# Causal attention on one core: VectorE's work placed behind TensorE's, a second part buffer, merged narrow steps, and products for the maxima issued twice

## The reference, cut to what matters

```python
B, L, D, H = (32, 64, 512, 32)     # x itself is (2, 1024, 512)
HD = D // H
q = (x @ Wq.T + bq).reshape(b, l, h, hd).transpose(0, 2, 1, 3)
k = (x @ Wk.T + bk).reshape(b, l, h, hd).transpose(0, 2, 1, 3)
v = (x @ Wv.T + bv).reshape(b, l, h, hd).transpose(0, 2, 1, 3)
scores = jnp.einsum('bhqd,bhkd->bhqk', q, k) / math.sqrt(hd)
scores = jnp.where(causal, scores, -jnp.inf)
att = jax.nn.softmax(scores, axis=-1)
out = jnp.einsum('bhqk,bhkd->bhqd', att, v)
out = out.transpose(0, 2, 1, 3).reshape(b, l, d) @ Wo.T + bo
```

## Time and profile before

| | us |
|---|---|
| median of three runs | 4300.12 (4286.41 to 4308.26) |
| the profiled execution, in all | 4294.83 |
| its span | 4293.1 |
| TensorE busy | 3861.4 (90%) |
| VectorE busy | 2711.2 (63%) |
| GpSimd busy | 1880.8 (44%) |
| ScalarE busy | 1695.2 (39%) |
| mean granted TensorE clock | 0.907 of full |
| attention, first batch (first projection to last turn) | 29.2 to 477.2 |
| attention, second batch | 2173.7 to 2617.4 |

### The profile page before, as it was taken

One profiled execution on the slowest core, in us unless ns is written; L12 is line 12 of the kernel. 1 busy time (PEld: TensorE's weight loads), 2 busy tenths in 40 slices (PEclk: granted clock), 3 DMA queues, 4 the chain that ended last, 5 costly groups with the idle time before them and its releaser, 6 DMA issues.

```text
span 4293.1 us, 61464 instructions
## 1 busy us (share of the span) xinstructions
PE 3861.4 (90%) x18056; PEld 2813.5 (66%) x18056; DVE 2711.2 (63%) x5034; ACT 1695.2 (39%) x3538; POOL 1880.8 (44%) x2017
## 2 busy tenths in 40 slices
PE   7899799689999999979878896996899999999797
PEld 4444478567777777757654444885677777777576
DVE  3567445577777777764435673555777777777644
ACT  1344411355545555541113444113555555555411
POOL 1111344355555655654311113443555556655542
PEclk8677899899999999989977767998999999999899
DMA  3221011011100111001032210110101001110010
GB/s 73 36 36 31 24 51 45 22 33 30 32 20 25 34 32 29 22 15 45 35 81 36 36 32 29 46 45 22 35 28 32 20 25 34 32 29 22 15 52 35
DMA packets 81456, 145.59 MB, mean 34 GB/s; under 512 B 16392, under 2 KB 18520, under 8 KB 81264
## 3 DMA queue, kind: packets, MB, share of 16 engines
q1 hardware_dynamic: 81264, 143.28, 12.9%
HBM read 113.08 MB, written 4.19 MB: 27 GB/s over the span
## 4 chain that ended last, share of the span: by engine, by line
PE 69%; issue 11%; DVE 7%; ACT 4%; POOL 3%; DVEq 2%; POOLq 2%; DMA 1%; SPq 1%; ACTq 0%
PE banks L492 15%; PE banks L493 14%; PE banks L494 14%; PE banks L832 4%; PE banks L671 4%; PE banks L652 3%; PE banks L628 3%; PE banks L825 2%; PE banks L845 2%; DVE conv L1344 2%; DVEq L1347 1%; PE banks L767 1%; PE banks L768 1%; POOL X L1509 1%; ACT conv L1005 1%
## 5 line engine op out<-in xcount | busy, mean ns | idle before, releaser
L1344 DVE SCALAR_TENSOR_TENSOR conv<-banks,cpar,conv 128x509 f32<-128x509 f32 (+2 forms) x576 | 428.2, 744 | 115.3 <-ACT conv L1005 100.9
L948 ACT ACTIVATE probs<-banks 128x1024 f32<-128x1024 f32 (+3 forms) x384 | 297.7, 810 | 309.4 <-PE banks L652 308.9
L1172 DVE TENSOR_TENSOR Y<-banks,Y 128x512 f32<-128x512 f32 x400 | 276.1, 691 | 188.1 <-PE banks L494 187.9
L1608 POOL TENSOR_SCALAR_AFFINE_SELECT probs<-probs 128x256 f32<-128x256 f32 x256 | 104.2, 408 | 645.8 <-ACT probs L948 645.5
L628 PE MATMUL banks<-stack_k,stack_q 48*128 48x512 f32 (+3 forms) x768 | 331.7, 502 | 59.3 <-DVEq L1218 19.8
L1672 POOL TENSOR_TENSOR state<-state,gt 128x512 f32<-128x512 f32 x112 | 133.5, 1192 | 500.4 <-PE banks L825 500.4
L492 PE MATMUL banks<-xhi,f_hi 128*128 128x512 f32 x800 | 322.6, 403 | 3.5 <-DVE xlo L1143 3.5
L492 PE MATMUL banks<-xhi,wx_hi 128*128 128x512 f32 x768 | 312.0, 406 | 14.4 <-DVE conv L1344 14.4
L493 PE MATMUL banks<-xhi,f_lo 128*128 128x512 f32 x800 | 319.9, 400 | 0.0
L494 PE MATMUL banks<-xlo,f_hi 128*128 128x512 f32 x800 | 319.4, 399 | 0.0
L494 PE MATMUL banks<-xlo,wx_hi 128*128 128x512 f32 x768 | 306.0, 398 | 0.0
(11 more groups left out here) (209 smaller groups left out, 10185.0 us busy)
## 6 DMA issues: line engine op xcount, KB each, us to landing
m_raw<-in_w_mamba SPq DMA_DIRECT2D x224, 256.0 KB, 2.6
f_raw<-in_w_ffn SPq DMA_DIRECT2D x50, 768.0 KB, 4.5
stack_q<-part_hi SPq DMA_DIRECT2D x128, 64.0 KB, 2.4
stack_k<-part_hi SPq DMA_DIRECT2D x128, 64.0 KB, 2.5
X<-in_x SPq DMA_DIRECT2D x4, 1024.0 KB, 6.5
wqk_raw<-in_w_attn SPq DMA_DIRECT2D x8, 512.0 KB, 3.5
stack_q<-part_lo SPq DMA_DIRECT2D x64, 64.0 KB, 2.4
stack_k<-part_lo SPq DMA_DIRECT2D x64, 64.0 KB, 2.5
```

Of the source, the lines that this page charges most:

```text
L948: act.activation(probs[n % 2][:, 2 * p:2 * p + 2, 0:w], banks[:, 2 * p:2 * p + 2, 0:w], ACT.Exp, scale=1.0 / HD ** 0.5).then_inc(exp_done[ ...
L1172: dve.tensor_tensor(Y[:, i, :], bank[6 + i % 2], Y[:, i, :], ALU.add).then_inc(f["dn_used"], 1)
L1344: r = dve.scalar_tensor_tensor(out=rest, in0=src[:, 0:HALF - lag], scalar=cpar[:, o:o + 1], in1=rest, op0=ALU.mult, op1=ALU.add)
```

## The change

Seven edits in attention, made together.

1. STEPS: the last two key tiles of each half become one step, with both tiles' scores side by side in one bank (`blocks`), one exponential and two masks: ten steps a quad instead of twelve.
2. VectorE's and ScalarE's parts get entries of their own (`proj_hi`, `proj_lo`, `values_out`, `maxima_out`, `turn_out`) that stand later in the order than TensorE's; a projection is issued in two halves of six matmuls in two consecutive steps. Banks are assigned ahead (`ring_banks`), and each use waits for the release of what that bank held last; before the first scores seven banks take part instead of three.
3. The parts get a second buffer, in the memory of X; x is loaded again at the end of attention, and POOL waits for that before it adds.
4. Projections move: the two of k of f = 1 from before the first scores into quad 0, those of f = 2 into quads 0 and 1, those of f = 3 into quads 2 and 3 (`PROJ_STEPS`).
5. Each head's stack DMAs have a semaphore of their own, and TensorE waits per head. SP's list is reordered: `stack(t + 1)` before `put_maxima(t)`.
6. From quad 1 on every piece is issued twice in a row, with the same operands into the same bank; in quad 7, which has no pieces to go with, every score is.
7. `maxima t + 1` still comes in the last step but one, pieces are dealt out over ten steps.

The diff, cut to its core:

```diff
-                part_hi = sb("part_hi", [P, 2, L], F32R, stack=s2)
-                part_lo = sb("part_lo", [P, 2, L], F32R, stack=s2)
+                part_hi = [sb("part_hi", [P, 2, L], F32R, stack=s2)[:]]
+                part_lo = [sb("part_lo", [P, 2, L], F32R, stack=s2)[:]]
+                for part, h in ((part_hi, 0), (part_lo, 1)):
+                    own = X[:, h * CPH:(h + 1) * CPH, :].rearrange("p (w u) d -> p w (u d)", w=2)
+                    part.append(own.bitcast(F32R))
...
-        STEPS = [(s, j) for s in range(2) for j in range(CPH * (s + 1))]
+        STEPS = [(s, (j,) if j < CPH * (s + 1) - 2 else (j, j + 1)) for s in range(2) for j in range(CPH * (s + 1) - 1)]
...
+        MAIN_BANKS, FIRST_BANKS = (4, 5, 7), (4, 5, 7, 0, 1, 2, 3)
+        for f, use, t, n in ((1, 2, 0, 0), (1, 3, 0, 2), (2, 0, 0, 6), (2, 1, 1, 0), (2, 2, 1, 3), (2, 3, 1, 6),
+                             (3, 0, 2, 2), (3, 1, 2, 6), (3, 2, 3, 0), (3, 3, 3, 4)):
+            PROJ_STEPS[t, n], PROJ_STEPS[t, n + 1] = (f, use, 0), (f, use, 1)
...
             for use in range(4):
-                yield "proj", 0, use
-            for i in range(5):
+                yield from project(0, use)
+            for i in range(2):
                 yield "values_in", i
+                yield "values_out", i
             for n in range(NP):
-                if n in (3, 9, 15):
-                    yield "values_in", 5 + (n - 3) // 6
-                if n in (21, 27, 33, 39):
-                    yield "proj", 1, (n - 21) // 6
-                yield "piece", 0, n
+                if n % 6 == 3 and n < 36:
+                    yield "values_in", 2 + n // 6
+                if n % 6 == 2 and 2 < n < 42:
+                    yield "values_out", 1 + n // 6
+                if n in (36, 40, 43, 46):
+                    yield "proj", 1, int(n > 40), int(n in (40, 46))
...
                     for q in range(QUAD):
                         yield "score", t, n, q
                         if n == NS - 2 and q == 1 and t + 1 < NQ:
                             yield "maxima", t + 1
+                        turning = n == NS - 2 and q < 2 and t + 1 < NQ
+                        more = n < NS - 2 and q == 0 or n in (0, 4) and q == 2
+                        yield from some(0 if turning else 2 if more else 1)
+                        if n == NS - 2 and q == 2 and t + 1 < NQ:
+                            yield "maxima_out", t + 1
+                        if q == 1 and n == 3 and t > 0:
+                            yield "turn_out", t - 1, 1
+                        if q == 1 and n == 7:
+                            yield "turn_out", t, 0
+                        if q == 2 and (t, n - 2) in PROJ_STEPS and PROJ_STEPS[t, n - 2][2]:
+                            yield "proj_lo", *PROJ_STEPS[t, n - 2][:2]
                     if n > 0:
                         yield "values", t, n - 1
-                    if n == 1 and t > 0:
+                    if n == 2 and t > 0:
                         yield "turn", t - 1, 1
-                    if n == 7:
+                    if n == 6:
                         yield "turn", t, 0
...
 # TensorE
-                        pe.wait_ge(ring_free, b * RING + ring - 2)
-                        r = pe.matmul(dst[:, 0:cols], stack_q[buf][base:base + ROWS, h, i * P:(i + 1) * P],
-                                      stack_k[buf][base:base + ROWS, h, s * HALF:s * HALF + cols],
-                                      start=True, stop=True)
+                        if i == 0:
+                            pe.wait_ge(stacked[t % 2][h], (b * (NQ // 2) + t // 2 + 1) * STACKED)
+                        bank_free(BEFORE[use])
+                        for _ in range(1 if t == 0 else 2):
+                            r = pe.matmul(bank[RING_BANK[use]][:, 0:cols],
+                                          stack_q[buf][base:base + ROWS, h, i * P:(i + 1) * P],
+                                          stack_k[buf][base:base + ROWS, h, s * HALF:s * HALF + cols],
+                                          start=True, stop=True)
...
+                        for j, lo, at, w in blocks(n) * (2 if t == NQ - 1 else 1):
+                            r = pe.matmul(bank[h][:, at:at + w],
...
 # SP
-                stack(0)
-                stack(1)
-                load_qk(1)
-                held(sp, v_used, b + 1)
-                ones_in(1)
-                put_maxima(0)
-                load_qk(2)
+                load_qk(1)
+                stack(0)
+                stack(1)
+                put_maxima(0)
+                load_qk(2)
+                held(sp, v_used, b + 1)
+                ones_in(1)
                 stack(2)
...
+                for t in range(2, NQ):
+                    if t + 1 < NQ:
+                        stack(t + 1)
                     put_maxima(t)
...
+                for par in range(2):
+                    for h in range(QUAD):
+                        held(sp, stacked[par][h], (b + 1) * (NQ // 2 * STACKED))
+                load_x(b)
                 leave(sp, b, ATT)
...
 # POOL
-            def add_normed(e, e_next):
+            def add_normed(e, e_next, b=None):
                 for i in range(TT):
+                    if b is not None and i % CPH == 0:
+                        held(pool, x_in[i // CPH], b * 32 + 32)
```

More of the change, by code:

```diff
@@ L299, in attention_order @@
+                if n == 45:
+                    yield "proj_lo", 1, 0
+                yield from some(1)
+            yield "maxima", 0
+            yield from some(2)
+            yield "maxima_out", 0
+            yield from some(2)
+            yield "proj_lo", 1, 1
+            yield from some(AHEAD - 4)
             for t in range(NQ):
@@ new lines, in build, with release @@
+        FREES = [o for o in ORDER if o[0] in FREED.values()]
+        FREE = len(FREES)
+        def release(use):
+            kind, *arg = use
+            if kind == "proj":
+                return "part_lo_ready", 4 * arg[0] + arg[1] + 1, ORDER.index(("proj_lo", *arg[:2]))
+            if kind == "maxima":
+                return "mt_ready", arg[0] + 1, ORDER.index(("maxima_out", *arg))
+            end = (FREED[kind], *arg)
+            return "ring_free", FREES.index(end) + 1, ORDER.index(end)
@@ new lines, in ring_banks @@
+        def ring_banks():
+            last, bank_of, before = {}, {}, {}
+            for use in RING_USES:
+                started_at = ORDER.index(use)
+                main = started_at >= ORDER.index(("score", 0, 0, 0))
+                allowed = MAIN_BANKS if main else FIRST_BANKS
+                k = min(allowed, key=lambda i: (last[i][2] if i in last else -1))
+                bank_of[use[:3]], before[use[:3]] = k, last.get(k)
+                last[k] = release(use)
+                if not main:
+                    first_scores = dict(last)
+            return bank_of, before, first_scores
```

254 lines of the change are left out of this document (126 added, 128 removed).

## The result

The changed kernel takes 4531.22 us (median of 4 runs, 4528.72 to 4535.9) against 4299.14 beside it: a ratio of 1.053, interval [1.051, 1.055], slower by 5.3%, where 4150 us and faster was forecast. The profiled execution has a span of 4529.8 us.

A forecast was written before the change was run, and what follows sets the result against it. A quad was taken as paced by VectorE for 14 us at full clock and TensorE for 27 at half. Terms sum to -74.5 us a batch, -149 for two: 4294.8 to 4146, median 4150 us, range 4065 to 4275.

The forecast's parts named there:

- The opening, -36 us a batch: Up to the first maxima mark: at 87 us instead of 122.8, so -36 us a batch, bounds -42 and -24.
- Removed: VectorE's stops at turns, projections and maxima, since each of its parts now stands a step later in the order.: Plain quads: VectorE's stops vanish, its work stays 28.5 us; with the copies, three such quads give -18.5 us a batch.
- the copies fill TensorE's gaps: Plain quads: 48 second copies, 8 us a quad, run beside products on other rows, supposing the clock stays up.
- the clock falls in every quad: Rival, first two steps of each quad: half clock as now, plain quads 49.5 us, total 4375 us; chance 0.10.
- 34 us for a plain quad at full clock: Quads without projections: 34 us each in place of 38.1 to 41.3, bounds 30 and 39.
- Quads 1 and 3 at 42 and 40 us: Three and two projections of 2.8 us on a 34 us base, in place of 60.6 and 57.9: -18 us each.
- Quad 0 +7, quad 2 +7: Quad 0 grows to 47 us with three projections, quad 2 to 48 with two and POOL's split: +7 each.
- The wait for POOL's split: Quad 2, before its first projection: TensorE waits 5 us for POOL to split new weights, now 1.72 us.
- Quad 7 +2 us, bounds 0 and 6: Last quad: doubled scores outrun ScalarE's exponentials with nothing else to fill in, +2 us, bounds 0 and +6.
- The load of a copy, put at 0.01 us: TensorE's matmuls: loading new weights shows with about 0.01 us, so 48 copies add under 1 us a quad.
- The rival with bare weights: Copies in seven quads: each pays a 0.187 us load, 4 us more a quad, total 4205 us; chance 0.08.
- the estimate's 5.1 us a quad: By the skill's 107 ns weight load, 48 copies add 5.1 us to a quad, total 4221 us.

The follow-up runs named there:

- e4_banks: Changed kernel, copies kept, with each projection whole in one step and its second part read out one step sooner: 4425.62 us, 1.028 of the kernel before.
- e9_dealt_late: Changed kernel with short bank holds, pieces twice, quad 7's scores once, and pieces dealt four to each of three first steps, then six: 4285.2 us, 0.993 of before.
- e6_short_twice: Changed kernel with projections whole and released sooner, turns read out at once, pieces still twice, quad 7's scores once: 4369.82 us, 1.015 of the kernel before.
- e5_short_single: Changed kernel with projections whole and released sooner, turns read out at once, every product issued once: 4258.53 us, 0.989 of the kernel before.
- e11_spread: Before's twelve-step main loop, changed opening, pieces twice, with ten main-loop projections dealt three, three, two, two to quads 0 to 3: 4224.02 us, 0.984 of before.
- e8_hybrid_twice: Changed kernel's opening and second buffer with before's twelve-step main loop, pieces of quads 1 to 7 issued twice: 4225.93 us, 0.983 of the kernel before.
- e7_hybrid_single: Changed kernel's opening and second buffer with before's twelve-step main loop, each product issued once: 4240.3 us, 0.985 of the kernel before.
- e2_before_twice: Kernel before with one edit, each piece from quad 1 on issued twice: 4324.44 us, 1.004 of the kernel before.
- e3_wide: Changed kernel with the first of each piece's two issues replaced by a 128-row product that the piece overwrites: 4903.6 us, 1.138 of the kernel before.
- e1_single: Changed kernel with every product issued once, order, banks and merged steps as changed: 4405.97 us, 1.023 of the kernel before.

## Why the prediction was wrong, point by point

- **The opening, -36 us a batch: right.** 86.7 against 87 forecast, in every kernel with edit 2's opening 86.7 to 89.7. The first score product starts at 92.7 us, forecast near 92. TensorE was busy 35.16 of 36.70 us at full clock, so the seven banks overlapped almost perfectly.
- **The step that failed first: "Removed: VectorE's stops at turns, projections and maxima, since each of its parts now stands a step later in the order."** It counted what a later entry spares VectorE, and not that the entry is also what frees the bank. With three banks, a projection that keeps one for three steps leaves two to pieces for most of quads 0 to 3, and TensorE and VectorE take turns. Priced by e4_banks at 106 us with copies; both holds together at 147 us without. Of the 106 us some are the clock's, which rose in quads 0 to 3 as well. In the forecast this term had the other sign, and no rival had it.
- **The step that failed second: "the copies fill TensorE's gaps", and the clock stays up.** The prediction named it as the step it trusted least and put a rival to it, *the clock falls in every quad*, with 0.10. That mechanism came true. The place that it named, the first steps without value products, fits e9_dealt_late, where fewer early pieces keep the clock up, but the trace of the changed kernel can't show it: there the clock is down in nearly all of quads 4 and 5. What spoke against this rival was misread: the products with V use all 128 rows too, and rows 5 have them at 426.71 and 430.86 us, within the slow stretch. Its price was too low. It made a plain quad 49.5 us; they took 55.4 to 59.6, and the total 4531 in place of 4375, since the rival had the clock alone. With the holds short the copies gave 47.4 to 53.8 us (e6_short_twice) and a total of 4370, about what the rival had worked out, though its three plain quads come to 28 us more than before and not 25.
- **34 us for a plain quad at full clock: nearly right**, 35.6 to 36.2 wherever the clock held. Only the condition wasn't met.
- **Quads 1 and 3 at 42 and 40 us:** 68.8 and 65.7. Without long holds and copies they take 54.5 and 47.8 (e5_short_single). So even then 12.5 and 7.8 us were missing, at clocks of 0.84 and 0.93. The clock isn't all of it: quad 3 of e9_dealt_late takes 46.9 us at 1.00. Its base was 36 and not 34, a projection cost 3.6 us, where 2.8 was taken (e11_spread against e8_hybrid_twice), and its stretch holds 35 matmuls of projections, nearly three projections, where two were counted: the last one of quad 2 is issued at the mark. 36 + 3 x 3.6 = 46.8 us.
- **Quad 0 +7, quad 2 +7:** they are 25 and 30 us longer than before. In e5_short_single they are 46.9 and 51.6, against the forecast's 47 and 48, so these terms fell with the two steps above; but the nearness is partly luck, since that kernel has no copies, clocks of 0.71 and 0.70, and two projections in quad 0's stretch where three were counted. The wait for POOL's split was 2.4 us, where 5 was taken.
- **Quad 7 +2 us, bounds 0 and 6: wrong.** It grew by 26. The doubled scores account for 13 to 19 of it in the first batch (58.8 and 64.7 against 45.7 in e6_short_twice), since at half clock they add TensorE's time straight to the quad. The other 13 are there in most kernels with the scores once, where quad 7 has a mean clock of 0.52 to 0.63 in place of 0.95, 0.70 in e7_hybrid_single. Kernels of twelve steps show both, e11_spread 33.1 us at 0.90, e8_hybrid_twice 45.6 at 0.57 and, in its second batch, 33.7 at 0.90: it is the clock, and merging isn't needed for it.
- **The load of a copy, put at 0.01 us: wrong.** In quads 4 to 6 of e8_hybrid_twice, at full clock, a piece of 512 columns and its copy start 0.31 to 0.34 us apart in 48 of 72 cases, where the columns take 0.21; 15 are at 0.23 to 0.24. Over all 48 pairs of a quad a copy takes 0.24 us and not 0.17, 0.08 of it above its columns: 3.8 us a quad. The next rows show one such pair, a score beside each. The Trainium skill, TensorE: Matmul & The Clock Gate, section LDWEIGHTS, gives about 107 ns for a load of 128 columns; the trace agrees with it in those two thirds, 0.10 to 0.13 us above the columns. The rival with bare weights had the mechanism right, at 0.187 us a copy. Of the estimate's 5.1 us a quad, 3.8 are there in TensorE's time. How much of them is in the quad's length (36 us and not 34) no run shows, since none has a quad at full clock without copies, and why these loads show and those between 600 and 700 us don't stays open.

```profile
292.75 0.49 PE L741 MATMUL banks<-stack_q,stack_k 50*128 50x512 f32 x1
292.75 0.49 PE L716 MATMUL banks<-stack_k,stack_q 48*128 48x512 f32 x1
293.08 0.39 PE L741 MATMUL banks<-stack_q,stack_k 50*128 50x512 f32 x1
293.08 0.39 PE L716 MATMUL banks<-stack_k,stack_q 48*128 48x512 f32 x1
```

The sum of the errors: plain quads +71, quads 1 and 3 +53, quads 0 and 2 +42, quad 7 +23 make 189 us a batch, 378 for two, and 4150 + 378 = 4528.

**What stays open.** What exactly makes the clock fall or hold isn't settled. The runs show that dealing the pieces late and giving banks back early together let it hold, that wide products don't raise it, and that the same program can go either way (e9_dealt_late's three groups, one quad of e2_before_twice up in one batch and down in the other). That the steps without products with V are too light for the clock is argued from the order of the work, not shown.

## What to carry to other kernels

Before a consumer's step is moved later so that it never waits, count the buffers: its entry is also the release, and with a ring of three, one buffer held for three steps costs more than the stop did. Work issued twice to hold a clock must be priced at both levels, as its cost comes due just when it fails. Take an edit of seven parts apart before believing its sum: here the opening gave some 66 us, and late releases, copies and quad 7's doubled scores together took 273 (after against e5_short_single).

## What was not expected of the hardware

- TensorE stayed at 1.2 GHz with hardly a gap in its records: 78.3 us with 76.84 busy in the changed kernel, 177.8 us with none idle in e3_wide. The Trainium skill, TensorE: Matmul & The Clock Gate, Part 1, has the level follow how busy TensorE is and puts the loss down to idle gaps; no gap between the records explains these rows.
- The clock goes two ways in one program: quad 6 of e2_before_twice takes 35.8 us in one batch and 47.8 in the other.
- A matmul of 48 rows and its copy run beside a score product of 50 rows on the other half of the array; with 48 copies a plain quad takes 36 us at the full level, less than the 38 to 41 without them at a mean clock of 0.67 to 0.78, and 10.5 us more than without them near the lower one (59.6 us in the changed kernel's quad 4, 49.1 in e1_single's).
